# Moving four steps of the first stage and of the scan's turn to other places in their engines' orders

## The reference

```python
xn = _layernorm(x)
x = x + mamba(xn) + moe_ffn(xn)          # layer 0
xn = _layernorm(x)
x = x + attention(xn) + moe_ffn(xn)      # layer 1

# mamba
proj = u @ W_in.T
z, x, B_toks, C_toks, dt_toks = split(proj)
xBC = silu(causal_conv(concat([x, B_toks, C_toks]), conv_w, taps=4) + conv_b)
dA = exp(softplus(dt_toks + dt_bias) * A)
S = S * dA_t + dt_t * B_t x_t ;  y_t = S C_t        # for each token
y = (y + D_param * x) * silu(z) ;  return y @ W_out.T

# moe_ffn: a shared network plus the two best of 8 experts
shared_out = silu_and_mul(x @ shared_gate_up) @ shared_down
topk_w, topk_i = top_k(softmax(x @ gate_w), 2)
```

## Time and profile before

| | us |
|---|---|
| median of 3 runs | 1523.24 (1514.99 to 1524.38) |
| the profiled execution, its own time | 1502.72 |
| its span, first to last instruction | 1501.2 |
| PE busy | 1392.2 (93%) |
| DVE busy | 828.9 (55%) |
| POOL busy | 657.1 (44%) |
| ACT busy | 512.8 (34%) |
| PE's share of the chain that ended last | 78% |
| mean granted clock of PE | 0.980 |

### The profile page before, as it was taken

One profiled execution on the slowest core, in us unless ns is written; L12 is line 12 of the kernel. 1 busy time (PEld: TensorE's weight loads), 2 busy tenths in 40 slices (PEclk: granted clock), 3 DMA queues, 4 the chain that ended last, 5 costly groups with the idle time before them and its releaser, 6 DMA issues.

```text
span 1501.2 us, 29754 instructions
## 1 busy us (share of the span) xinstructions
PE 1392.2 (93%) x10881; PEld 1133.1 (75%) x10881; DVE 828.9 (55%) x2307; ACT 512.8 (34%) x1102; POOL 657.1 (44%) x814
## 2 busy tenths in 40 slices
PE   7999999999999999899998899999999988888886
PEld 6888889999999999666665566666666557777775
DVE  4556434444444444588888677777777623322256
ACT  2212122222222222333332455555545443333331
POOL 2355423333333332554443245445444455666561
PEclk9999999999999999999999999999999999999998
DMA  5894921111111111500000110111100012222357
GB/s 183 145 116 66 93 62 50 47 47 50 50 50 47 47 50 36 172 1 0 0 0 22 44 43 23 44 36 30 44 23 16 2 30 73 86 85 85 108 187 234
DMA packets 69936, 94.89 MB, mean 63 GB/s; under 512 B 13401, under 2 KB 57433, under 8 KB 69808
## 3 DMA queue, kind: packets, MB, share of 16 engines
q1 hardware_dynamic: 51152, 53.92, 16.3%
q0 software_dynamic: 18656, 39.23, 8.4%
HBM read 60.66 MB, written 32.44 MB: 62 GB/s over the span
## 4 chain that ended last, share of the span: by engine, by line
PE 78%; DVE 9%; issue 6%; another core or an unknown queue 3%; POOL 2%; ACT 1%; DMA 0%; DVEq 0%; POOLq 0%; ACTq 0%
PE score L1657 47%; PE mixed L1657 18%; PE side L1657 8%; PE side L1873 2%; DVE ARENA L1406 2%; DVE WGU L1499 2%; PE side L1667 1%; POOL ARENA L731 1%; PE mixed L2047 1%; DVE stats L1061 1%; PE side L2040 1%; DVE X L1614 1%; DVE X L1524 1%; DVE ARENA L1390 0%
## 5 line engine op out<-in xcount | busy, mean ns | idle before, releaser
L757 POOL DMA_INDIRECT XN<-xn_rows,slot_tok x111 | 108.6, 978 | 233.0 <-PE side L1873 205.5
L1657 PE MATMUL score<-xT,HT 128*128 128x128 f32 x1136 | 208.0, 275 | 0.0
L764 POOL DMA_INDIRECT y_rows<-sh_gu,slot_row x149 | 146.3, 982 | 125.6 <-ACT sh_gu L941 89.8
L792 POOL TENSOR_SCALAR_AFFINE_SELECT ARENA<-ARENA 128x256 f32<-128x256 f32 x256 | 104.5, 432 | 193.7 <-ACT ARENA L973 193.1
L1499 DVE TENSOR_REDUCE WGU<-score 128x2 f32<-128x256 f32 (+1 forms) x256 | 130.8, 553 | 104.8 <-PE score L1657 101.9
L1657 PEld LDWEIGHTS score<-xT,HT 128*128 128x128 f32 x1136 | 166.8, 192 | 0.0
L1288 DVE TENSOR_TENSOR HT<-sh_gu,score 128x128 f32<-128x128 f32 (+1 forms) x149 | 71.2, 478 | 146.7 <-issue 74.6
L973 ACT ACTIVATE ARENA<-score 128x768 f32<-128x768 f32 x128 | 103.8, 811 | 137.4 <-PE score L1657 137.0
L699 POOL DMA_INDIRECT lists<-token_no,w_in x128 | 125.1, 977 | 40.0 <-issue 28.5
L1657 PE MATMUL score<-ARENA 32*128 32x256 f32 (+1 forms) x2048 | 127.4, 355 | 14.1 <-DVE WGU L1499 8.1
L1263 DVE COPY xT<-WGU 128x256 f32 x142 | 45.6, 362 | 169.8 <-PE score L1657 169.0
(11 more groups left out here) (251 smaller groups left out, 2651.2 us busy)
## 6 DMA issues: line engine op xcount, KB each, us to landing
WGU<-in_gu SPq DMA_DIRECT2D x8, 1024.0 KB
WGU<-y_rows SPq DMA_DIRECT2D x32, 256.0 KB, 3.1
ARENA<-y_rows SPq DMA_DIRECT2D x32, 256.0 KB
xn_rows<-XN SPq DMA_DIRECT2D x24, 256.0 KB
X<-in_u SPq DMA_DIRECT2D x16, 256.0 KB
ARENA<-in_dn SPq DMA_DIRECT2D x8, 512.0 KB
out<-X SPq DMA_DIRECT2D x16, 256.0 KB
y_rows<-sh_gu,slot_row POOLq DMA_INDIRECT x149
```

What stands on the lines that cost most here:

```text
L757: x["got"][j % ring].mark(eng.indirect_dma_start(XG[j % ring], None, xn_rows[l], bass.IndirectOffsetOnAxis(slot_tok[:, j:j + 1], 0)))
L764: x["out"][j % RING].mark(eng.indirect_dma_start(y_rows[g], bass.IndirectOffsetOnAxis(slot_row[:, j:j + 1], 0), YO[j % RING], None))
L792: ins = eng.affine_select(out=m, in_=m, compare_op=ALU.is_ge, fill=0.0, base=0, pattern=[[0, 2], [1, P]], channel_multiplier=-1)
L1657: return eng.matmul(o, l, r, start=start, stop=stop)
```

## The change

Nothing is computed otherwise, and no instruction is added or taken away. Each engine's code is written in another order, with the waits that this needs:

1. First stage, DVE: in a turn with two fronts, `front_stats` and `front_apply` of the second front stand ahead of `add_down` and of the first front's `front_pick`.
2. First stage, turn 3: PE does `ffn_up` of sequence 0 ahead of the transposes of sequence 1, and ACT its silu ahead of their copies.
3. Scan, DVE: a turn is `gate_y`, `conv_silu`, `add_y`, `scan_parts`, `conv_taps(new)`, `z_silu`. It was `gate_y`, `conv_taps(conv)`, `scan_parts`, `conv_silu`, `add_y`, `z_silu`. The taps of a sequence are so done in the turn in which it is projected.
4. Scan, ACT: `conv_tanh` ahead of `decays`, and `conv_first` ahead of `state_copy` and `z_tanh`.
5. Scan, PE: part 4 of the projection stands first in the turn, behind the wait for `cv` of the sequence before; parts 2 and 3 stand behind `turn_parts`. Turns 1 and 2 are written out otherwise: in turn 1 the projection stands ahead of the first `decay_sums`, in turn 2 the first `turn_parts` ahead of the projection.
6. Scan, POOL: a turn waits first for `xs` of the new sequence, then does `carry_factors`, the first piece of the decay matrix, and, behind a new wait for `wm` of the sequence before, the other two pieces.

```diff
--- before.py
+++ after.py
@@ -726,6 +726,8 @@
 
             if pieces[0] == 0:
                 M["dec"].wait(eng, r.n, 1)
+            elif pieces[0] == 1:
+                M["wm"].wait(eng, r.n, 1)
             for a in pieces:
                 av = DT3[:, a, bass.ds(r.n * CH, CH), :].rearrange("p c h -> p (c h)")
                 ins = eng.tensor_tensor(
@@ -741,14 +743,14 @@
             M["ce"].mark(eng.tensor_tensor(CE, CE, CT[r.u][:, P:SEQ].unsqueeze(1).broadcast_to([P, MH // 2, P]), ALU.mult))
 
         def mamba(new, r):
-            ahead = new and not (isinstance(new.n, int) and new.n == 0)
+            ahead = new and r
             if ahead:
-                decay_factors(new, range(PIECES - 1))
+                M["xs"].wait(eng, new.n)
             if r:
                 carry_factors(r)
             if ahead:
-                M["xs"].wait(eng, new.n)
-                decay_factors(new, range(PIECES - 1, PIECES))
+                decay_factors(new, range(1))
+                decay_factors(new, range(1, PIECES))
 
         def gather_tile(l, j):
 
@@ -851,9 +853,11 @@
             if of(k - 2):
                 norm_stage(0, of(k - 2))
         for fronts, s, old in first_turns():
+            if s and s.n == 0:
+                ffn_silu(0, s)
             for k in fronts[:1]:
                 front(k)
-            if s:
+            if s and s.n:
                 ffn_silu(0, s)
             for k in fronts[1:]:
                 front(k)
@@ -911,16 +915,19 @@
             M["zt"].mark(act(ZT.rearrange("p k t -> p (k t)"), bank[1][:, :], ACT.Tanh, scale=0.5))
 
         def mamba(new, conv, r, old):
-            if r:
+            starting = r and conv and isinstance(r.n, int) and r.n == 0
+            if starting:
                 decays(r)
             if conv:
                 conv_tanh(conv)
+            if r and not starting:
+                decays(r)
+            if new:
+                conv_first(new)
             if r:
                 state_copy(r)
             if r:
                 z_tanh(r)
-            if new:
-                conv_first(new)
         def experts(l):
             x = EX[l]
 
@@ -1351,13 +1358,14 @@
                 gate_product(0, s, 3)
             if s and s.n == NSEQ - 1:
                 list_done(0)
+            for k in fronts[1:]:
+                front_stats(k)
+                front_apply(k)
             if old:
                 add_down(0, old)
             for k in fronts[:1]:
                 front_pick(k)
             for k in fronts[1:]:
-                front_stats(k)
-                front_apply(k)
                 front_logits(k)
                 front_pick(k)
             if s and s.n == NSEQ - 2:
@@ -1451,13 +1459,13 @@
             if old:
                 gate_y(old)
             if conv:
-                conv_taps(conv)
-            if r:
-                scan_parts(r)
-            if conv:
                 conv_silu(conv)
             if old:
                 add_y(old)
+            if r:
+                scan_parts(r)
+            if new:
+                conv_taps(new)
             if r:
                 z_silu(r)
         for t, stages in enumerate(tile_turns(NJ)):
@@ -1749,11 +1757,13 @@
                 rank_tokens(0, NSEQ // 2 - 1)
 
         for fronts, s, old in first_turns():
+            if s and s.n == 0:
+                eng.wait_ge(s_sh0, 16)
+                N[0]["xT"].wait(eng, 0)
+                ffn_up(0, s)
             for k in fronts[:1]:
                 front_turn(k)
-            if s:
-                if s.n == 0:
-                    eng.wait_ge(s_sh0, 16)
+            if s and s.n:
                 ffn_up(0, s)
             for k in fronts[:1]:
                 front_route(k)
@@ -1847,15 +1857,23 @@
                 carried(c)
 
         def mamba(new, conv, r, old):
-            if r:
+            at = new.n if new and isinstance(new.n, int) else None
+            if new and at != 0:
+                if at == 2:
+                    turn_parts(r)
+                M["cv"].wait(eng, new.n, 1)
+                project(new, (4,))
+            if at == 1:
+                M["proj"].mark(project(new, (2, 3)))
+                decay_sums(of(0))
+            if r and at != 2:
                 decay_sums(r)
             if old:
                 project_y(old)
-            if r:
+            if r and at != 2:
                 turn_parts(r)
-            if new and not (isinstance(new.n, int) and new.n == 0):
-                M["cv"].wait(eng, new.n, 1)
-                M["proj"].mark(project(new, (2, 3, 4)))
+            if new and at != 0 and at != 1:
+                M["proj"].mark(project(new, (2, 3)))
             if r:
                 state(r)
                 if not (isinstance(r.n, int) and r.n == 0):
```

## The result

In 20 runs each the changed kernel took 1532.33 us (median; 1522.02 to 1558.67) and the kernel before 1517.03 (1507.58 to 1532.32). The ratio is 1.0085, with a 95% interval of 1.0057 to 1.0113: 13 us slower (8.6 to 17.1), under the 1% that I called telling, but not nothing. The ratio leaves out the three runs of the changed kernel (1546.77, 1552.52 and 1558.67) that took over 1.5% more than its fastest; the medians of all twenty are 15.3 apart. I had forecast +0.5 us, and 1523.7 from a base of 1523.24: the base itself came out 6.2 lower in twenty runs. The profiled execution took 1522.02 (span 1520.4), against 1502.7 (1501.2).

What follows compares the result with a forecast made beforehand. PE was taken to bound the first stage, and a ring through PE and DVE's taps the scan. First stage -11 and scan +11.5 gave +0.5 on 1523.24, so 1523.7 us, range 1506 to 1539.

Steps and rivals of the forecast that it cites:

- Scatters and loads so start about 11 us earlier, and I expect the landing to follow: First stage's end: earlier rows of sequence 15 let down-weight loads and POOL's scatters start earlier; -11 us, ends 0 and -12.
- The first rival: First stage gives nothing back, as lists are ready only when the DMA engines have emptied; 1535 us, chance 0.13.
- some tenths: First stage, turn 3: edit 2 could gain some tenths of a us and lose as much; taken as 0.
- The ring: Scan turn: part 4, decay sums, `project_y`, `turn_parts`, parts 2 and 3, `conv_first`, taps, next part 4; 13.25 us, 0.6 longer.
- twelve turns: Scan's steady turns, from the start of sequence 3 to that of 15: 13.25 us each instead of 12.65.
- The scan's sum: Whole scan, its start, twelve turns, end and POOL's contention together: +11.5 us, ends +8 and +14.
- start, to the first of the twelve turns: Scan's start: projection of sequence 3 begins at 635.5 instead of 637.69, 2.2 us earlier.
- POOL beside `scan_parts`: Scan's two ends: a POOL piece beside `scan_parts` adds 0.5 to 1.2 us in each of two turns; +1 taken.
- a rival of 0.09: Scan: PE's clock falls in the new 1.25 us gap each turn, 13 turns cost 22 us more; 1546, chance 0.09.
- its two products of that kind would be stretched each turn: Scan: if contention held each turn, `scan_parts`' two-SBUF-input products stretch 0.55 us and more, yet end before `conv_first` at 9.3.
- The sum: Whole kernel: -11 us in the first stage and +11.5 in the scan give +0.5 us.
- the case that I had held likeliest: Whole kernel: the change does what it says and both stages gain as counted; 1515 to 1531 us, chance 0.64.

Runs made afterwards that it cites:

- e3_part4: Changed kernel with PE's part 4 of the projection moved behind the decay sums in steady scan turns; 1.0058 of the kernel before, 12.72 us a turn.
- e9_fill: Changed kernel with five added useless matmuls on PE ahead of part 4's wait for the taps in steady turns; 1.0146 of the kernel before.
- e10_nowm: Changed kernel without POOL's wait for `wm`; 1.0173 of the kernel before.
- e6_pool: e3_part4 with POOL's order from before the change and no wait for `wm`; 1.0244 of the kernel before, 15.1 us a turn.
- e2_scan: Changed kernel with edits 1 and 2 undone, so the scan's edits alone; 1.0130 of the kernel before, 19 us slower.
- e5_cover: Changed kernel with PE's whole projection behind the decay sums, ahead of `turn_parts` and `project_y`, `add_y` behind `z_silu`, POOL's old order; 1.0292 of the kernel before.

## Why the prediction was right and where it was not

**Edit 1** came out in the case's trace as counted, step by step: wait, clock, last store, landing, list (-10.8 for -11). It did not come out in the medians. Alone it measured +1.9 us (-1.5 to +5.3) on one chip and -3.8 (-9.2 to +1.5) on another. The step that failed is "Scatters and loads so start about 11 us earlier, and I expect the landing to follow", read as true of every execution. Two things are seen in the traces that can hide it: rows held up because their buffer was still being stored (16.1 us in one wait of PE), and a remainder of the stage that varies from 72 to 89 us. Why that remainder varies stays open. The first rival, with its 0.13, was set too low: no profile shows a stage that gains nothing, but two medians show less than half of the 11, by their middles.

**Edit 2** was never measured alone. In the case's trace PE is 0.37 us later behind it, which is of the size of the "some tenths" that I weighed against each other and took as 0.

**The ring** is the one predicted, in its order and length (13.40 for 13.25). e3_part4 shows it by taking one member out. In twelve turns the missing 0.15 makes 1.8 us.

**The scan's sum** was +11.5 and measured +20.7. Three terms were mis-sized, by landmarks:

| | forecast | measured |
|---|---|---|
| start, to the first of the twelve turns | -2.2 | +0.1 |
| twelve turns | +7.2 | +12.6 |
| end, from the projection of 15 to attention's first store | +5.4 | +8.0 |
| POOL beside `scan_parts`, counted apart | +1 | in the lines above |

The largest is the clock, which I had at nothing in the forecast and at 22 us in a rival of 0.09. It was neither. By the granted clock, 20.4 us of the changed scan passed at 1.2 GHz, and 3.4 of the one before; with half the work done in such a time, the most that this can cost is (20.4 - 3.4) / 2 = 8.5 us. On the path it was some 6: +3.6 in the two long turns, +1.7 in the turn of 15 (taps to taps, 15.05 for 13.40), and +0.7 in the projection of 1 at the start (5.14 for 4.40; it stands behind a wait of 4.18 in both kernels and takes 4.33 to 5.46 over all profiles, so this part isn't the change's). e9_fill shows for the steady turns, in one execution, that the gap brings the slow stretches on; for the turn of 15 it is only argued. The second term is POOL beside `scan_parts`: I took +1 from a row of 0.96, and it was 1.7 at the start (2.09 for 0.41) and 0.6 at the end (1.11 for the 0.51 that it took before the change). The third is the ring's 0.15 a turn, 1.8. Together that is 10.1, or 9.1 without the 1 that was counted; 20.7 - 11.5 is 9.2.

The Trainium skill's page TensorE: Matmul & The Clock Gate, on its second failure mode (short pauses, each turn anew, make the clock swing), is borne out in kind: with a gap of 1.34 us each turn the granted clock over nine turns is 0.99, with one of 0.64 it is 1.00. I gave its rival the wrong form, each turn or never; in the table, e10_nowm aside, the clock falls as the gap grows. The Trainium skill's page GPSIMD Engine Reference, section 1 (SBUF interfaces shared with VectorE), is borne out more strongly than I used it: by 1.7 us for one product.

**The POOL edit** I called free. In steady turns of the changed kernel it is: PE waits there for the taps alone. e10_nowm and e6_pool show what it is for. The step "its two products of that kind would be stretched each turn" and still end in time held only because of that wait.

**The sum.** +0.5 was forecast and +13 measured. Both errors have one sign, so they don't cancel. The median of 1532.33 is 1 us above the case that I had held likeliest (1515 to 1531). That it still lies in the range of 1506 to 1539 is partly luck: the upper end was there for a first stage without gain, not for the clock, and the base fell by 6.2. The scan cost 19 to 21 in each place where it was seen (20.7, 20.1, e2_scan's 19 in the median) for 11.5; if it did in the twenty runs too, the 13 leave some 7 for the first stage, of 11 (an estimate from these differences; no run measures it).

## What to carry to other kernels

When a dependence is cut out of a loop, write down the new ring with every instruction that the moved one is queued in front of: moving the consumer to the head of its engine's queue puts the whole queue in the ring. Before an order is changed on PE, list what each step hides for others (here `project_y` hid ACT's copies, z hid the state's copy), since that wait appears the moment the cover goes. And look at which engines share SBUF at the new place, not only at how long each step took at the old one.

## What the runs showed of the hardware that I had not expected

A GpSimd product over bf16 tiles of 128x1024 (1.89 us) beside a VectorE product with two SBUF operands stretches the latter from 0.41 to as much as 2.1 us: in the changed kernel's scan it ends 0.28 us behind the GpSimd instruction, whenever it began. Taps that read one operand from a bank keep their 3.85. And the clock's answer to gaps is not all or nothing: 0.64 us each turn left it at 1.00, 1.34 lengthened two turns of twelve (0.99), and gaps of 1.7 to 3.1 us, one each turn of 15.1 us, in e5_cover and e6_pool left it at 0.95 and 0.94. Each of these is one execution.
